# A fused attention and mixture-of-experts kernel: other landing times and due times in its planner, and a second half for the buffer of the attention sums

## The chip, the cores and the metric

The kernel runs on one core of a Trainium2 chip. The metric is the device time of one execution in microseconds (us). The kernel before has a median of 1803.69 us in three runs (1797.37 to 1806.76).

## The reference, cut to what matters

The input x is 8 sequences (the kernel calls each a batch n) of 1024 tokens with 256 features, all in float32. One pre-norm transformer layer is computed:

```
x = x + attention(layernorm(x))      # 16 heads of 16, causal softmax, probabilities times a gate per key
x = x + ffn(layernorm(x))            # 8 experts of width 128, two chosen per token, plus shared experts of width 256

attention: Q, K, V = x@Wq+bq, x@Wk+bk, x@Wv+bv
           gate = tanh(gelu(gelu(norm(x@dp_w1)) @ dp_w2 ...) ...)   # one number per key
           out = (softmax(mask(Q K^T / 4)) * gate) V ; out @ Wo + bo
ffn:       scores = sigmoid(x @ gate_w.T); 4 groups of 2 experts; the best 2 groups; the best 2 experts of these
           y = sum over the two of weight * (silu(x w1) * (x w3)) w2 ; plus the shared experts
```

## The kernel before, in words

Work is cut by batch (n, 8), by group of four heads (g, 4) and by half of the sequence (c, 2 "chunks" of 512 queries). The stages of a batch are: projection (layer norm on DVE, POOL and ACT, transposes and the Q, K and V products on PE), the gate, and for each group first the row maxima of the scores (items M, on DVE the reduce at L1549 and L1546), then the scores again with the maximum subtracted (QK, L1941), their exponential on ACT (EX, L1358), the causal mask on POOL (MK, L1175) and the sums over keys (PV, L1961). The maxima go through a small transfer (SM, L972) into the query tile. Sums are copied from PSUM to `o_sb` by ACT (OE, L1369) and stored to DRAM by SP (SO, L978). After the four groups of a half the row sums are loaded (CL, L986), inverted, stored (CV, L990), and quarters of 256 tokens are loaded (CO, five transfers, L1004 to L1007), multiplied on POOL (CP, L1184), projected (CW, L1970), normalised (CS to CN), transposed (CT, L1978) and handed to the router (CG, L1993), the shared experts and the chosen experts (EU L2071, HT L2081, ED L2102). Tokens are scattered to slots of their experts by indirect transfers from POOL (SX, L1207), slots are loaded in pairs (XL, L1023), worked on, copied to `ysb` by ACT (YC, L1448) and stored (YS, L1033). At the end each tile of 128 tokens gathers its two results (GY, L1219), loads the rest (RL, L1042, tile `rr`), is scaled on ACT (CM, L1294), added on POOL (CB L1227, CC L1232) and stored (SY, L1046). The last batch has no slots: every expert runs on every quarter.

Nothing of this order is written out by hand. `Plan.run` draws it up before the program is built. Every item is added by `plan_work` with its engine, its duration in ns, the items it comes after, its due time and, for a transfer, `lands`: the time from the end of its issue to the point where the plan lets others use the data. The plan goes through time; on each engine it takes, of the items that could start now, the one with the earliest due time. Each engine then runs its items strictly in that order and waits on semaphores, so an order that rested on a landing that comes later than planned makes an engine wait with other work queued behind. `LATER` adds a number of ns to the due time of each kind of item. PE has three ways of tiling (FULL 128x128, ROWS 64x128 for M and QK, COLS 128x32 for PV). The plan charges `SWITCH` for a change of tiling, and `EXPOSED` more unless the new one is COLS; an item in another tiling than the last has `SAME_TILING` added to its due time, so that items of one tiling are kept together. [...] Where the plan sees PE idle with sums open, `keep_busy` puts small matmuls (L858).

```
HEARD = {"PE": {"PE": 0, "ACT": 37, ...}, ...}       # ns until another engine sees an item's end
ISSUE = 620                                          # ns of one transfer's issue on SP
seen[item] = now + ns + (TAIL[e] if lands is None else lands)
cost = [f[1] + (SAME_TILING if f[2] and f[2] != tiling else 0) for f in found]
```

`rank_op` (L1604 to L1615) gives each of n values its rank among n: it compares all with all in a cube of tiles x n x n, five DVE instructions one after the other. `choose_op` calls it twice, for 4 group scores and for 8 expert scores; once per batch for 8 tiles, and in the last batch once per quarter for 2 tiles.

Of the kernel before, what the change touches and what calls it, by code (L numbers as in the profile page):

```python
# [79 lines left out]
RANK_OP = 13  # L80
# [20 lines left out]
DENSE_OPS = 19  # L101
# [8 lines left out]
SWITCH, EXPOSED = 100, 90  # L110
PERIOD, KEEPS = 3413, 0.58
SAME_TILING = 12000
# [65 lines left out]
def max_parts(u):  # L178
# [3 lines left out]
    for qt in qts:  # L182
# [7 lines left out]
LATER = {"AC": 8000, "AQ": -1000, "AX": 7000, "CB": 6000, "CC": -41000, "CG": 3000, "CJ": 2000, "CL": -8000,  # L190
# [138 lines left out]
def plan_work():  # L329
# [11 lines left out]
    def projection(n):  # L341
# [3 lines left out]
        for h in range(HALVES):  # L345
# [3 lines left out]
                lands=4500 if n else 2600, early=70_000 if n == 1 else 0)  # L349
# [59 lines left out]
    def maxima(n, g):  # L409
# [3 lines left out]
        for c in range(CHUNKS):  # L413
# [74 lines left out]
    def quarter(n, q):  # L488
# [4 lines left out]
        if q % (QS // CHUNKS) == 0:  # L493
            early = at(n + 1) - (GROUP_T * 0.4 if c == 0 else 0)
            add("SP", ("CL", n, c), ISSUE, early, [("SO", n, g, c) for g in range(GROUPS)] + [("CV", n - 1, c)], lands=3500)
            add("DVE", ("CR", n, c), 980, early, [("CL", n, c)])
            add("SP", ("CV", n, c), ISSUE, early, [("CR", n, c)], lands=2600)
# [30 lines left out]
        add("SP", ("SR", n, q), ISSUE, begin + 9000, [("FD", n, q)], lands=3500)  # L528

    def routing(n):  # L530
        begin = at(n + 1) + T * SHARE_TO - 10000
        for r, step in enumerate(ROUTE[n]):
            ns = 620 if step in range(9, RANK_OP + 1) else 150
# [10 lines left out]
    def pair(n, u):  # L544
# [4 lines left out]
        add("SP", ("XL", n, u), ISSUE, due - 6000, [("SX", n, 2 * TILES - 1), ("XT",) + back], lands=3500)  # L549
# [6 lines left out]
        add("SP", ("YS", n, u), ISSUE, due + 3500, [("YC", n, u)], lands=3000)  # L556

    def mix(n):
        last = SETS[SET_OF[n]][-1]
        begin = pair_due(last, PAIR_COUNT[last]) + T * MIX_LONG * SETS[SET_OF[n]].index(n)  # L560
        for t in range(TILES):
# [3 lines left out]
            add("SP", ("RL", n, t), ISSUE, due - 3000, [("SR", n, t // QT), ("SY",) + back], lands=2600)  # L565
# [4 lines left out]
            add("SP", ("SY", n, t), ISSUE, due, [("CC", n, t)], lands=2600)  # L570
# [60 lines left out]
def build(nc, ins, out):  # L631
# [4 lines left out]
    with ExitStack() as ctx:  # L636
# [75 lines left out]
        o_sb = sb("o_sb", [P, CHUNK])  # L712
# [14 lines left out]
        cmp_b = sb("cmp_b", [P, TILES, EXPERTS, EXPERTS])  # L727
# [12 lines left out]
        slot_f = sb("slot_f", [P, 2, TILES])  # L740
        slot_u = sb("slot_u", [P, 4, 2, TILES], mybir.dt.uint32)
        owner, owner_old = sb("owner", [P, SLOT_TILES]), sb("owner_old", [P, SLOT_TILES])
        owner_i = sb("owner_i", [P, 2, SLOT_TILES], mybir.dt.int32)
        share = sb("share", [P, 2, TILES])
# [134 lines left out]
        def _(sp):  # L879
# [95 lines left out]
            def store_o(item, n, g, c):  # L975
                b, k = release["OE", n, g, c]
                sp.wait_ge(freed[b], k)
                sp.dma_start(o_s[bass.ds((n * GROUPS + g) * P, P), c * CHUNK:(c + 1) * CHUNK], o_sb[:]).then_inc(o_st[c], 16)  # L978
# [270 lines left out]
        def _(act):  # L1249
# [110 lines left out]
            def copy_o(item, n, g, c):  # L1360
# [8 lines left out]
                nc.scalar.copy(o_sb[:], bank(("PV", n, g, first))).then_inc(freed[release[item][0]], 1)  # L1369
# [95 lines left out]
        def _(dve):  # L1465
# [135 lines left out]
            def rank_op(r, v, n_v, to, ts):  # L1601
                a, b_ = cmp_a[:, ts, 0:n_v, 0:n_v], cmp_b[:, ts, 0:n_v, 0:n_v]
# [8 lines left out]
                if r == 2:  # L1611
                    return nc.vector.tensor_tensor(b_, other, mine, ALU.is_gt)
                if r == 3:
                    return nc.vector.tensor_tensor(a, a, b_, ALU.add)
                return nc.vector.tensor_reduce(to, a, X_AXIS, ALU.add)  # L1615

            def choose_op(r, ts):
# [9 lines left out]
                if r < 8:  # L1627
                    return rank_op(r - 3, grp[:, ts, :], EXPERTS // 2, rank_g[:, ts, :], ts)
                if r == 8:
# [4 lines left out]
                return rank_op(r - 9, sel[:, ts, :], EXPERTS, rank[:, ts, :], ts)  # L1634
# [15 lines left out]
            def slot_op(n, step):  # L1650
# [58 lines left out]
                return nc.vector.tensor_copy(slot_u[:, n % 4, :, :], slot_f[:])  # L1709

            def owner_op(n, step):
# [10 lines left out]
                if step in ("owner_old", "owner"):  # L1722
                    return nc.vector.tensor_reduce((owner_old if step == "owner_old" else owner)[:], ends, X_AXIS, ALU.add)
                if step == "within":
                    return nc.vector.scalar_tensor_tensor(out=owner_old[:], in0=owner_old[:], scalar=float(EXPERTS),
                                                          in1=owner_old[:], op0=ALU.is_lt, op1=ALU.mult)
                if step == "both":
                    return nc.vector.tensor_tensor(owner[:], owner[:], owner_old[:], ALU.add)
# [416 lines left out]
```

## Time and profile before

| | before |
|---|---|
| runs, median (lowest to highest) | 1803.69 us (1797.37 to 1806.76) |
| the profiled execution | 1808.59 us |
| its span on the core | 1806.6 us |
| mean granted TensorE clock | 0.962 of full |
| PE busy | 1653.0 us, 91% of the span |
| DVE, ACT, POOL busy | 1292.4, 1081.9, 811.8 us (72%, 60%, 45%) |
| all transfers | 261.25 MB, mean 145 GB/s |

The span is the time from the first to the last instruction of the profiled execution; 2.0 us lie around it. Busy is the time in which an engine has an instruction in work. The chain that ended last is read backwards: from the last instruction to what released it, and so on; of the span 54% of that chain are PE's, 14% DVE's, 8% each those of transfers, ACT and POOL, 5% issue. A piece of the chain called DMA starts when its transfer is issued and ends when it has landed.

### The profile page before, as it was taken

What the parts mean: (1) busy time and instruction counts of PE and PEld (TensorE: products, weight loads), DVE (VectorE), ACT (ScalarE), POOL (GpSimd) and SP (SyncE); (2) the same over time, 40 slices, a digit from 0 to 9 for tenths busy, and PEclk for the clock granted to TensorE, in tenths of its full rate; (3) what the DMA queues carried; (4) which work ended last, traced back from release to release, by engine and by line L of the source; (5) the groups of instructions that cost most, each with busy time, mean ns of one, the idle gap of its engine ahead of it and who ended that gap; (6) DMA issues with size and microseconds to landing.
All of it is one profiled execution on the core that took longest, in us unless ns stands there. A gap on an engine that the chain in (4) does not pass through costs nothing.

```text
span 1806.6 us, 34673 instructions
## 1 busy us (share of the span) xinstructions
PE 1653.0 (91%) x12785; PEld 982.5 (54%) x12785; DVE 1292.4 (72%) x2528; ACT 1081.9 (60%) x1808; POOL 811.8 (45%) x1390
## 2 busy tenths in 40 slices
PE   7798989989988999899998989999999889999888
PEld 3344446435544566455654555555564557666677
DVE  5776767967795777777785757877688666963655
ACT  3466756665655655675656755586556765568432
POOL 5234533463345221632237863363207773157760
PEclk9699999999998999999998999999999999999999
DMA  5556655554445532644545665453535675336440
GB/s 151 158 156 194 176 169 152 182 153 124 125 127 147 158 104 87 174 113 120 159 118 151 185 194 152 127 162 108 147 93 172 198 197 159 97 129 199 135 122 13
DMA packets 192708, 261.25 MB, mean 145 GB/s; under 512 B 19616, under 2 KB 127264, under 8 KB 192544
## 3 DMA queue, kind: packets, MB, share of 16 engines
q1 hardware_dynamic: 181792, 229.67, 44.0%
q0 software_dynamic: 10752, 29.37, 5.6%
q8 instruction: 105, 1.72, 0.4%
q14 instruction: 59, 0.48, 0.1%
HBM read 130.98 MB, written 127.40 MB: 143 GB/s over the span
## 4 chain that ended last, share of the span: by engine, by line
PE 54%; DVE 14%; DMA 8%; ACT 8%; POOL 8%; issue 5%; SPq 3%; another core or an unknown queue 0%; POOLq 0%; ACTq 0%; DVEq 0%
PE ps_all L1961 10%; PE ps_all L2071 10%; DVE mx L1549 7%; PE ps_all L1941 6%; PE ps_all L1908 6%; PE ps_all L2102 5%; PE ps_all L1892 4%; ACT probs L1358 4%; PE ps_all L1878 3%; PE ps_all L1970 3%; POOL xs_s L1207 2%; PE ps_all L2081 2%; PE ps_all L2034 1%; DMA rr<-r_s 1%; DMA out<-rr 1%
## 5 line engine op out<-in xcount | busy, mean ns | idle before, releaser
L1549 DVE TENSOR_REDUCE mx<-ps_all 128x2 f32<-128x1024 f32 (+2 forms) x640 | 619.0, 1006 | 132.5 <-PE ps_all L1908 74.4
L1358 ACT ACTIVATE probs<-ps_all 128x1024 f32<-128x1024 f32 x576 | 571.8, 1028 | 218.0 <-PE ps_all L1941 209.9
L1175 POOL TENSOR_SCALAR_AFFINE_SELECT probs<-probs 128x256 f32<-128x256 f32 (+1 forms) x448 | 190.9, 443 | 495.5 <-ACT probs L1358 491.3
L1961 PE MATMUL ps_all<-probs,vaug 128*32 128x512 f32 (+3 forms) x3072 | 319.4, 516 | 21.9 <-POOL probs L1175 15.3
L1908 PE MATMUL ps_all<-k_st,q_st 63*128 63x512 f32 (+3 forms) x1536 | 269.3, 401 | 48.0 <-ACT probs L1358 16.3
L1941 PE MATMUL ps_all<-q_st,k_st 64*128 64x512 f32 (+3 forms) x1536 | 265.6, 401 | 29.3 <-ACT probs L1358 9.9
L1908 PEld LDWEIGHTS ps_all<-k_st,q_st 63*128 63x128 f32 x1536 | 135.1, 193 | 163.7 <-issue 52.2
L1941 PEld LDWEIGHTS ps_all<-q_st,k_st 64*128 64x128 f32 x1536 | 130.9, 191 | 158.9 <-issue 67.2
L2071 PE MATMUL ps_all<-w_hi,x2h 128*128 128x512 f32 (+1 forms) x480 | 168.2, 350 | 4.3 <-DVE x2l L1598 2.5
L1804 DVE SCALAR_TENSOR_TENSOR act_t<-act_t,ps_all 128x256 f32<-128x256 f32 x168 | 70.4, 419 | 123.4 <-ACT act_t L1421 110.9
L2071 PE MATMUL ps_all<-w_lo,x2h 128*128 128x512 f32 (+1 forms) x480 | 157.0, 327 | 0.0
L2071 PE MATMUL ps_all<-w_hi,x2l 128*128 128x512 f32 (+1 forms) x480 | 157.0, 327 | 0.0
L1421 ACT ACTIVATE act_t<-ps_all 128x256 f32<-128x256 f32 x168 | 64.6, 385 | 151.3 <-PE ps_all L2071 122.2
L1961 PEld LDWEIGHTS ps_all<-probs,vaug 128*32 128x32 f32 x3072 | 73.2, 110 | 131.6 <-issue 89.4
L1207 POOL DMA_INDIRECT xs_s<-xnb,slot_u x112 | 111.6, 996 | 42.9 <-issue 39.8
L1219 POOL DMA_INDIRECT yab<-ys_s,slot_u x112 | 108.3, 967 | 33.0 <-issue 20.2
L2102 PE MATMUL ps_all<-w_hi,h_hi 128*128 128x256 f32 (+1 forms) x336 | 109.5, 326 | 7.7 <-DVE h_lo L1831 6.9
L2071 PEld LDWEIGHTS ps_all<-w_hi,x2h 128*128 128x128 f32 x480 | 90.8, 189 | 27.6 <-issue 19.7
L1878 PE MATMUL ps_all<-wvd,xt 128*128 128x384 f32 x256 | 96.9, 506 | 1.8 <-issue 0.9
L2071 PEld LDWEIGHTS ps_all<-w_hi,x2l 128*128 128x128 f32 x480 | 90.9, 189 | 8.4
L1831 DVE TENSOR_TENSOR h_lo<-ps_all,h_hi 128x256 fp32r<-128x256 f32 x168 | 70.0, 419 | 35.1 <-ACT h_hi L1436 32.7
L2102 PE MATMUL ps_all<-w_lo,h_hi 128*128 128x256 f32 (+1 forms) x336 | 94.3, 281 | 0.0
(195 smaller groups left out, 2849.8 us busy)
## 6 DMA issues: line engine op xcount, KB each, us to landing
qk_s<-qh SPq DMA_DIRECT2D x116, 256.0 KB
q_st<-qk_s SPq DMA_DIRECT2D x128, 192.0 KB
k_st<-qk_s SPq DMA_DIRECT2D x128, 192.0 KB
xs<-xs_s SPq DMA_DIRECT2D x72, 256.0 KB
ys_s<-ysb SPq DMA_DIRECT2D x72, 256.0 KB
o_s<-o_sb SPq DMA_DIRECT2D x64, 256.0 KB
qk_s<-ql SPq DMA_DIRECT2D x57, 256.0 KB
xs_s<-ysb SPq DMA_DIRECT2D x20, 512.0 KB, 6.0
```

Of the source, the lines that this page charges most:

```text
L1175: last = nc.gpsimd.affine_select(out=block, in_=block, compare_op=ALU.is_ge, fill=0.0, base=0, pattern=[[0, heads], [1, P]], channel_multi ...
L1207: nc.gpsimd.indirect_dma_start(xs_s[i % 2], bass.IndirectOffsetOnAxis(ap=slot_u[:, n % 4, a, t:t + 1], axis=0), xnb[:, t, :], None).then_i ...
L1219: nc.gpsimd.indirect_dma_start(yab[:, t % 2, a, :], None, ys_s[SET_OF[n] % 2], bass.IndirectOffsetOnAxis(ap=slot_u[:, n % 4, a, t:t + 1], ...
L1358: nc.scalar.activation(to, of, ACT.Exp, scale=DH ** -0.5).then_inc(freed[release[item][0]], 1)
L1549: last = nc.vector.tensor_reduce(to[:, :, p, qt % QPC], both[:, :, at:at + keys], X_AXIS, ALU.max)
L1878: last = mm(bank(item)[:, 0:E + DP], xt[:, k, tt * P:(tt + 1) * P], wvd[:, k, :], start=(k == 0), stop=(k == KE - 1))
L1892: last = mm(bank(item), w[:, k, m * P:(m + 1) * P], xt[:, k, :], start=(k == 0), stop=(k == KE - 1))
L1908: last = mm(bank(item, j)[:, to:to + keys], q_st[r, q_half(n, g, c), p, qt % QPC * P:(qt % QPC + 1) * P], k_st[r, k_half(n, g, kc), p, 0:k ...
L1941: last = mm(bank(item, j)[:, to:to + cols], k_st[r, k_half(n, g, kt // QPC), a, kt % QPC * P:(kt % QPC + 1) * P], q_st[r, q_half(n, g, c), ...
L1961: last = mm(bank(first)[32 * h:32 * h + 32, q0 - c * CHUNK:], vaug[:, kt, g, h * VW:h * VW + 32], probs[:, s % 2, h, at:at + cols], start= ...
L2071: last = mm(bank(item)[:, to], x[:, buf, k, t * P:(t + 1) * P], w[:, k, cs], start=(k == 0 and j == 0), stop=(k == KE - 1 and j == 2))
L2102: last = mm(bank(first)[:, t * E:(t + 1) * E], h[:, z % 2, i * P:(i + 1) * P], w[:, cs], start=(item == first and i == 0 and j == 0), stop ...
```

## The change

It has four parts.

1. Constants of the plan. `lands` of nine kinds of transfer goes up: x (AX) 4500 to 5500, maxima (SM) 2600 to 3600, sums (SO) 6000 to 6400, row sums in (CL) 3500 to 4600 and out (CV) 2600 to 3600, rest out (SR) 3500 to 4500, slots in (XL) 3500 to 5200, slots out (YS) 3000 to 4600, rest in and result out (RL, SY) 2600 to 4300. A change of tiling costs 114 instead of 100 and 104 instead of 90 ns more, `SAME_TILING` is 14000 instead of 12000, `KEEPS` 0.6 instead of 0.58.
2. `LATER` has other numbers, and 35 more kinds of item in it (77 in place of 42); among the larger moves: the gate (GA, GD) 13 and 10 us earlier, RL 10 earlier, SY and CL 12 earlier, CC 10 earlier, SM 12 later, XL 10 later, GL 21 later, WF 18 later. The order of the work on all five engines comes out of these two parts.
3. `o_sb` has two halves, one per chunk. The copy of a half waits for the store of the same chunk one group earlier, instead of for the store just before it.
4. `rank_op` reduces each comparison by itself and adds the small results: six instructions in place of five, so that `cmp_b` needs two tiles in place of eight; `slot_f`, `share` and `owner_old` lie in `cmp_a` and `cmp_b`. That makes room for the half of part 3.

```diff
-RANK_OP = 13
+RANK_OP = 15
-DENSE_OPS = 19
+DENSE_OPS = 21
-SWITCH, EXPOSED = 100, 90
-PERIOD, KEEPS = 3413, 0.58
-SAME_TILING = 12000
+SWITCH, EXPOSED = 114, 104
+PERIOD, KEEPS = 3413, 0.6
+SAME_TILING = 14000
-LATER = {"AC": 8000, "AQ": -1000, "AX": 7000, "CB": 6000, "CC": -41000, "CG": 3000, "CJ": 2000, "CL": -8000,
+LATER = {"AB": 8000, "AC": 15000, "AE": 22000, "AG": -1000, "AN": 4000, "AQ": -1000, "AR": -5000, "AS": -1000,
...
-                lands=4500 if n else 2600, early=70_000 if n == 1 else 0)
+                lands=5500 if n else 2600, early=70_000 if n == 1 else 0)
-            add("SP", ("SM", n, g, c), 2 * ISSUE, due, [("MN", n, g, c)], lands=2600)
+            add("SP", ("SM", n, g, c), 2 * ISSUE, due, [("MN", n, g, c)], lands=3600)
-                [("SO", (u - 1) // (GROUPS * CHUNKS), (u - 1) // CHUNKS % GROUPS, (u - 1) % CHUNKS)] if u else []),
+                [("SO", (u - 2) // (GROUPS * CHUNKS), (u - 2) // CHUNKS % GROUPS, c)] if u >= CHUNKS else []),
-            add("SP", ("SO", n, g, c), ISSUE, due + 4000, [("OE", n, g, c)], lands=6000)
+            add("SP", ("SO", n, g, c), ISSUE, due + 4000, [("OE", n, g, c)], lands=6400)
...
-        add("SP", ("YS", n, u), ISSUE, due + 3500, [("YC", n, u)], lands=3000)
+        add("SP", ("YS", n, u), ISSUE, due + 3500, [("YC", n, u)], lands=4600)
-            add("SP", ("RL", n, t), ISSUE, due - 3000, [("SR", n, t // QT), ("SY",) + back], lands=2600)
+            add("SP", ("RL", n, t), ISSUE, due - 3000, [("SR", n, t // QT), ("SY",) + back], lands=4300)
-            add("SP", ("SY", n, t), ISSUE, due, [("CC", n, t)], lands=2600)
+            add("SP", ("SY", n, t), ISSUE, due, [("CC", n, t)], lands=4300)
...
-        o_sb = sb("o_sb", [P, CHUNK])
+        o_sb = sb("o_sb", [P, CHUNKS, CHUNK])
-        cmp_b = sb("cmp_b", [P, TILES, EXPERTS, EXPERTS])
+        cmp_b = sb("cmp_b", [P, 2, EXPERTS, EXPERTS])
...
-                if c:
-                    act.wait_ge(o_st[0], (gi + 1) * 16)
-                else:
-                    act.wait_ge(o_st[1], gi * 16)
+                if gi:
+                    act.wait_ge(o_st[c], gi * 16)
...
                 if r == 2:
-                    return nc.vector.tensor_tensor(b_, other, mine, ALU.is_gt)
+                    return nc.vector.tensor_reduce(to, a, X_AXIS, ALU.add)
                 if r == 3:
-                    return nc.vector.tensor_tensor(a, a, b_, ALU.add)
-                return nc.vector.tensor_reduce(to, a, X_AXIS, ALU.add)
+                    return nc.vector.tensor_tensor(a, other, mine, ALU.is_gt)
+                if r == 4:
+                    return nc.vector.tensor_reduce(others, a, X_AXIS, ALU.add)
+                return nc.vector.tensor_tensor(to, to, others, ALU.add)
```

## Rows read from the trace of the kernel before

**Rows 1.** The page, part 1: busy us of each engine (share of the span) xinstructions.

```profile
PE 1653.0 (91%) x12785; PEld 982.5 (54%) x12785; DVE 1292.4 (72%) x2528; ACT 1081.9 (60%) x1808; POOL 811.8 (45%) x1390
```

**Rows 2.** Who PE's matmuls waited for: us in total, times, longest us.

```profile
PE ps_all L1908 <- ACT probs L1358: 16.3, 30, 1.9
PE ps_all L1908 <- DVE mx L1549: 14.5, 31, 1.9
PE ps_all L1941 <- ACT probs L1358: 9.9, 26, 1.6
PE ps_all L1941 <- DVE mx L1549: 9.7, 19, 1.9
```

**Rows 3.** Timeline, stalls of PE and two of other engines: start us, us, ..., idle before and releaser.

```profile
249.61 0.95 DVE L1561 RECIPROCAL rows_of<-rows_of 64x128 f32<-64x128 f32 x1 [3.98 <-DMA rows_of<-o_s]
...
251.88 0.80 PE L1941 MATMUL ps_all<-q_st,k_st 64*128 64x512 f32 x2 [1.85 <-DVE mx L1549]
...
1043.83 0.91 ACT L1294 ACTIVATE yab<-yab,wab 128x256 f32<-128x256 f32 x2 [4.19 <-DMA yab<-ys_s,slot_u]
...
1045.03 0.50 PE L1908 MATMUL ps_all<-k_st,q_st 63*128 63x512 f32 x2 [1.92 <-DVE mx L1549]
1052.29 0.51 PE L1908 MATMUL ps_all<-k_st,q_st 63*128 63x512 f32 x2 [1.92 <-ACT probs L1358]
...
1666.38 0.36 PE L2102 MATMUL ps_all<-w_hi,h_hi 128*128 x1 [1.75 <-DVE h_lo L1831]
1678.96 1.18 PE L1978 MATMUL ps_all<-ident,xnb 128*128 128x128 f32 x4 [4.86 <-ACT xnb L1315]
1742.51 0.97 PE L1978 MATMUL ps_all<-ident,xnb 128*128 128x128 f32 x3 [2.77 <-ACT xnb L1315]
```

**Rows 4.** The chain that ended last, its transfers there: start us, us until landed.

```profile
242.28 7.31 DMA rows_of<-o_s
...
1044.02 8.95 DMA rr<-r_s
...
1659.48 7.81 DMA ys_s<-ysb
1677.21 5.88 DMA rr<-r_s
1724.44 5.57 DMA rr<-r_s
```

**Rows 5.** Transfers by kind: count, KB each, median us from issue to landing.

```profile
r_s<-x SPq DMA_DIRECT2D x28, 256.0 KB, 2.8
```

**Rows 6.** Stretches: us; PE, PEld, DVE, ACT, POOL busy (x); PE clock, DMA share, GB/s.

```profile
240.00:260.00 20.00, 15.48 (x71) 7.55 (x72) 10.17 (x15) 9.22 (x13) 5.40 (x3) 0.83 0.66 186
...
1040.00:1060.00 20.00, 15.52 (x78) 7.34 (x76) 10.68 (x14) 8.39 (x14) 11.48 (x18) 0.84 0.69 183
...
1660.00:1680.00 20.00, 12.42 (x81) 8.02 (x81) 4.37 (x13) 9.42 (x19) 13.77 (x19) 0.87 0.59 166
...
1740.00:1760.00 20.00, 14.61 (x62) 10.72 (x63) 10.79 (x34) 5.99 (x16) 10.72 (x14) 0.83 0.37 111
```

**Rows 7.** Timeline, a store of the sums and the next copy, closest pair.

```profile
388.66 0.35 SPq L978 DMA_DIRECT2D o_s<-o_sb  x1
396.29 0.59 ACT L1369 COPY o_sb<-ps_all 128x512 f32<-128x512 f32 x1
```

**Rows 8.** DVE groups by form, the add and reduce of the rank: busy us, mean ns.

```profile
L1614 DVE TENSOR_TENSOR cmp_a<-cmp_a,cmp_b 128x512 f32<-128x512 f32 x7 | 4.9, 697 | 0.0
...
L1615 DVE TENSOR_REDUCE rank<-cmp_a 128x64 f32<-128x512 f32 x7 | 4.7, 678 | 0.0
```

**Rows 9.** Timeline of DVE, the same two in the last quarter: start us, us.

```profile
1755.74 1.26 DVE L1614 TENSOR_TENSOR cmp_a<-cmp_a,cmp_b 128x128 f32<-128x128 f32 x1
1757.04 0.29 DVE L1615 TENSOR_REDUCE rank<-cmp_a 128x16 f32<-128x128 f32 x1
```

**Rows 10.** Who PE's weight loads waited for: us in total, times, longest us.

```profile
PEld ps_all L1961 <- issue: 89.4, 320, 1.7
```

More of the change, by code:

```diff
@@ L494, in quarter @@
             early = at(n + 1) - (GROUP_T * 0.4 if c == 0 else 0)
-            add("SP", ("CL", n, c), ISSUE, early, [("SO", n, g, c) for g in range(GROUPS)] + [("CV", n - 1, c)], lands=3500)
+            add("SP", ("CL", n, c), ISSUE, early, [("SO", n, g, c) for g in range(GROUPS)] + [("CV", n - 1, c)], lands=4600)
             add("DVE", ("CR", n, c), 980, early, [("CL", n, c)])
-            add("SP", ("CV", n, c), ISSUE, early, [("CR", n, c)], lands=2600)
+            add("SP", ("CV", n, c), ISSUE, early, [("CR", n, c)], lands=3600)
         back = divmod(k - 2, QS)
@@ L527, in quarter @@
         add("DVE", ("FD", n, q), 600, begin + 9000, [("ED", n, q, quarter_units(n) - 1)], frees=(("ED", n, q, 0), None))
-        add("SP", ("SR", n, q), ISSUE, begin + 9000, [("FD", n, q)], lands=3500)
+        add("SP", ("SR", n, q), ISSUE, begin + 9000, [("FD", n, q)], lands=4500)
     def routing(n):
@@ L532, in routing @@
         for r, step in enumerate(ROUTE[n]):
-            ns = 620 if step in range(9, RANK_OP + 1) else 150
+            ns = 620 if step in range(10, RANK_OP + 1) else 150
             ready = [("RO", n, r - 1)] if r else [("RT", n, QS - 1), ("GY", n - 4, TILES - 1), ("CM", n - 4, TILES - 1)]
@@ L548, in pair @@
         y = look_of(n, QS, u)
-        add("SP", ("XL", n, u), ISSUE, due - 6000, [("SX", n, 2 * TILES - 1), ("XT",) + back], lands=3500)
+        add("SP", ("XL", n, u), ISSUE, due - 6000, [("SX", n, 2 * TILES - 1), ("XT",) + back], lands=5200)
         add("PE", ("XT", n, u), 370, due - 2000, [("XL", n, u)] + look_end(y - 2), 1, FULL)
@@ L1363, in copy_o @@
                     act.wait_ge(pv_done, gi * NSTEP + LAST_STEP[c] + 1)
-                if c:
-                    act.wait_ge(o_st[0], (gi + 1) * 16)
-                else:
-                    act.wait_ge(o_st[1], gi * 16)
+                if gi:
+                    act.wait_ge(o_st[c], gi * 16)
                 first = FIRST_STEP[c]
-                nc.scalar.copy(o_sb[:], bank(("PV", n, g, first))).then_inc(freed[release[item][0]], 1)
+                nc.scalar.copy(o_sb[:, c, :], bank(("PV", n, g, first))).then_inc(freed[release[item][0]], 1)
             def copy_hi(item, n, q, i):
@@ L1601, in rank_op @@
             def rank_op(r, v, n_v, to, ts):
-                a, b_ = cmp_a[:, ts, 0:n_v, 0:n_v], cmp_b[:, ts, 0:n_v, 0:n_v]
+                a, others = cmp_a[:, ts, 0:n_v, 0:n_v], cmp_b[:, 0, 0:ts.stop - ts.start, 0:n_v]
                 cube = [P, ts.stop - ts.start, n_v, n_v]
@@ L1633, in choose_op @@
                         scalar=2.0, in1=sc[:, ts, :].rearrange("p t (g o) -> p (t g) o", o=2), op0=ALU.is_lt, op1=ALU.mult)
-                return rank_op(r - 9, sel[:, ts, :], EXPERTS, rank[:, ts, :], ts)
+                return rank_op(r - 10, sel[:, ts, :], EXPERTS, rank[:, ts, :], ts)
             def spread_op(r, ts):
@@ L1722, in owner_op @@
                 if step in ("owner_old", "owner"):
-                    return nc.vector.tensor_reduce((owner_old if step == "owner_old" else owner)[:], ends, X_AXIS, ALU.add)
+                    return nc.vector.tensor_reduce(owner_old if step == "owner_old" else owner[:], ends, X_AXIS, ALU.add)
                 if step == "within":
-                    return nc.vector.scalar_tensor_tensor(out=owner_old[:], in0=owner_old[:], scalar=float(EXPERTS),
-                                                          in1=owner_old[:], op0=ALU.is_lt, op1=ALU.mult)
+                    return nc.vector.scalar_tensor_tensor(out=owner_old, in0=owner_old, scalar=float(EXPERTS),
+                                                          in1=owner_old, op0=ALU.is_lt, op1=ALU.mult)
                 if step == "both":
-                    return nc.vector.tensor_tensor(owner[:], owner[:], owner_old[:], ALU.add)
+                    return nc.vector.tensor_tensor(owner[:], owner[:], owner_old, ALU.add)
                 return nc.vector.tensor_scalar(owner_i[:, SET_OF[n] % 2, :], owner[:], float(EXPERTS - 1), float(2 * F),
```

14 lines of the change are left out of this document (7 added, 7 removed), and 14 rows, old and new, of the table LATER.

## The prediction

> **What bounds the kernel now.** I read the page first, then PE's waits, then the timeline around its longest stalls, and last the chain of work. The page says that PE is busy 1653.0 of 1806.6 us, far ahead of DVE at 1292.4 [rows 1]. So PE is the bound, and what can be won without taking work from it is its idle time, 1806.6 - 1653.0 = 153.6 us, and the time that it works at a low clock: at a mean granted clock of 0.962 the missing 0.038 is 1806.6 x 0.038 = 69 us. The idle time is not in one place. Of matmul waits, the four largest groups in which PE waits in its M and QK items for a bank that ACT or DVE has yet to empty sum to 16.3 + 14.5 + 9.9 + 9.7 = 50.4 us, in 106 waits of at most 1.9 us [rows 2].
>
> The timeline shows a second kind: an engine stands in its fixed order before a transfer that has not landed, and what is queued behind it comes late. At 249.61 DVE has waited 3.98 us for the row sums; the maxima behind them come late, and PE stalls 1.85 us at 251.88. At 1043.83 ACT has waited 4.19 us for gathered rows, and PE stalls 1.92 us twice soon after. At 1666.38, 1678.96 and 1742.51 PE stalls 1.75, 4.86 and 2.77 us [rows 3]. The chain shows transfers ahead of these: row sums landed 7.31 us after their issue began, a slot store 7.81, and loads of the rest 8.95, 5.88 and 5.57 [rows 4]. The plan of before expected, with 0.62 us of issue, 0.62 + 3.5 = 4.12 us for the first, 0.62 + 3.0 = 3.62 for the second and 0.62 + 2.6 = 3.22 for the others. This is what the change is about.
>
> **The change part by part.**
>
> *Landings.* After the change the plan expects 5.22, 5.22 and 4.92 us for these three kinds. Of the lateness it takes in (5.22 - 4.12) / (7.31 - 4.12) = 34% for the row sums, 1.6 / 4.19 = 38% for the slot store, 1.7 / 2.66 = 64% and 1.7 / 2.35 = 72% for the loads of the rest at 1677 and 1724 us [rows 4]. I let PE's stall behind each shrink by that share: 1.85 x 0.34 + 1.75 x 0.38 + 4.86 x 0.64 + 2.77 x 0.72 = 0.6 + 0.7 + 3.1 + 2.0 = 6.4 us, of 11.2 [rows 3]. The chain for the last two runs from the load of the rest over POOL's adds (L1227, L1232) and gathers to the layer norm of the quarter, all queued on POOL, and from there to ACT and PE. The two stalls at 1045 and 1052 stand behind a gather (GY), whose landing of 4000 ns is not changed: nothing is counted. Not every raise goes towards the trace: stores of the rest land after a median of 2.8 us, where the plan said 4.12 and now says 5.12 [rows 5]. That costs nothing by itself, since a semaphore is waited for and not a time; it only lets the plan put other work first. Ends: nothing comes back (0), or all 11.2 us.
>
> *The clock behind the stalls.* The stretches from 240, 1660 and 1740 us have granted clocks of 0.83, 0.87 and 0.83; a part of each ran at 1.2 GHz, the lower level, in place of 2.4 GHz, after PE had stood still [rows 6]. 20 us at 0.83 lose 3.4 us of full-speed work, so the three lose 3.4 + 2.6 + 3.4 = 9.4 us. With stalls shorter by 6.4 of 11.2 I take the same share of it, 5.4 us. Ends: 0 and 9.4 us. The stretch from 1040 us, 0.84, belongs to the gather and stays.
>
> *Two halves of the sums' buffer.* Before, the copy at L1369 waits for the store just before it. In all 64 pairs the closest is a store that starts at 388.66 and a copy that starts at 396.29, 7.6 us later, and ACT's idle time before L1369 is never ended by a transfer [rows 7]. So the wait that is removed costs 0 now. The plan, which holds the copy back for 0.62 + 6.0 us, may place it earlier, and with it the bank that it frees; PE's own waits on this copy are under 2 us in all, so I take 0, with 2 us to gain at the other end.
>
> *The rank in six instructions.* Each call gives up one add over the cube and gains a reduce over the same cube and a small add. At 8 tiles the add took 0.697 us and the reduce 0.678 [rows 8]; the small add is taken at the price of the short reduce, 0.29 us [rows 9]. So a call costs -0.02 + 0.29 = +0.27 us, 14 calls in seven batches +3.8 us on DVE, which has over 500 us to spare; it hides beside the maxima, and costs up to 3.8 us where DVE is just then the one PE waits for. In the last batch, 8 calls, the add over 2 tiles took 1.26 us and the reduce 0.29 while POOL was at work [rows 9], so a call gives back 1.26 - 0.58 = 0.68 us there and costs 0.3 where POOL is quiet. Sum on the path: 0, ends -5 and +4. On this pair of rows the Trainium skill has a rule ("SBUF — State Buffer", Who interferes with whom): a DVE instruction with two inputs in SBUF contends with a GpSimd instruction that reads SBUF, a reduce on trn2 does not. By it the part would be on the side of the gain, about -0.7 us in the only place where the router's chain holds PE; it changes the sum by less than 1 us.
>
> *Due times, costs of tiling and of the clock.* These reorder all engines: SP's queue (row sums, loads of the rest and results earlier, maxima later), POOL's (second add and the gate earlier) and ACT's. No work goes away. What is left of PE's idle time is 153.6 - 11.2 = 142 us, and a new order draws it anew. No row says in which direction. I take 0, with a fifth of it, 30 us, as the bound on either side: less than the 50.4 us of waits for banks [rows 2], which a new order moves first.
>
> Sum against the profiled execution: 1808.6 - 6.4 - 5.4 + 0 + 0 + 0 = 1796.8 us. It lies 4.9 us above the median of the three runs, so the forecast for the median is 1791.9, rounded to 1791 us.
>
> **The rivals.**
>
> *A. The stalls only move (no change).* PE's order is as rigid as before. Where the plan now allows for a landing of a row sum or a load, another kind whose landing is as low as it was (the gather, or the stores of Q and K) becomes the late one. For it: the wait of 4.19 us before the gather's use [rows 3]. Against it: at the three places that I count it is the raised kinds that lead the chain. It gives 1808.6 - 4.9 = 1804, 1795 to 1812.
>
> *B. Longer runs in one tiling (slower).* With 14 in place of 12 us of preference for the present tiling PE does more M or QK items in a row. One M item's PE time is about 0.5 us, its two reduces on DVE more than 1 us, so that each further item of a run waits for a bank. The place is the four groups of [rows 2]. If they grow by 80%, 40 us come on top, and the time is 1792 + 40 = 1832; the point from which it decides is a growth by (1804 - 1792) / 50.4 = 24%, over which the gain is eaten; at 50% it gives 1817. For it: these waits are the largest group already. Against it: the same plan counts the banks and sees a wait for them coming.
>
> *C. Fewer changes of tiling (a larger gain).* The timeline has some 1080 changes between the three tilings, the first at 37 us and the last at 1672 us. Before the PV items PE's weight loads stood still for 89.4 us in 320 waits with no releaser, 0.28 us each [rows 10]. If the new costs take away 10% of the changes, that is up to 108 x 0.28 = 30 us, and the time is 1762. Against it: much of that idle lies beside a matmul still running. The Trainium skill ("TensorEngine Tiling (Array Packing)", Key Properties) says that a change of the tiling mode drains the engine, which speaks for a full price of each change; no row here separates the drain.
>
> *D. The change does not do what it says.* The second half changes nothing where the wait was never met [rows 7]. That is in my sum already; if the landings were no cause either, the result is A.
>
> **How the numbers follow.** A measurement of this kernel can tell about 0.5%, 9 us, from no change: the bounds are 1794.7 and 1812.7. My forecast gets 0.43 (its own range 1780 to 1799: 0.35 of it under 1794.7, 0.08 within), C and a lucky redraw 0.19 (1755 to 1780), A 0.16 (within), B 0.22 (1813 to 1835). Faster by over 0.5%: 0.35 + 0.19 = 0.54; within: 0.08 + 0.16 = 0.24; slower: 0.22. For the range I leave out about a third of C at the lower end and half of B at the upper: 1768 to 1817. The likeliest case's own range is 1780 to 1799.
>
> **What would show it.** If I am right, the profile of the changed kernel has the stalls of PE before L1978 near the end shorter than 4.86 and 2.77 us, POOL's waits for loads of the rest and DVE's for row sums smaller in total, a granted clock of 0.965 or more, PE's busy time within 10 us of 1653, and no wait of ACT at L1369 for a transfer. A is right if these waits shrink and others grow by as much; B if the four groups of [rows 2] exceed 62 us; C if the weight loads' waits with no releaser before L1961 fall under 80 us. I am wrong if the redraw of all orders, which I put at 0, is the largest term: then the idle time of PE changes by more than 15 us with no landing at the head of it.

## The result, and the profile after

The changed kernel takes 1788.28 us (median of 11 runs, 1778.47 to 1798.91) against 1800.42 us for the kernel before (11 runs, 1793.26 to 1809.04). The ratio is 0.993, with a 95% interval of 0.9902 to 0.9959. A second measurement of the same program beside the kernel before (e9) gave 0.9928 (0.9902 to 0.9953). So the change is faster by 0.7%, near the 1791 us forecast; how much of that is owed to the reasons that I gave is what the experiments are about.

| | before | after |
|---|---|---|
| median of all runs | 1800.42 us | 1788.28 us |
| profiled execution | 1808.59 us | 1798.91 us |
| its span | 1806.6 us | 1797.1 us |
| PE busy, PE idle | 1653.0, 153.6 us | 1650.4, 146.7 us |
| granted clock | 0.962 | 0.968 |

Both profiled executions are slower than their medians, the changed one by 10.6 us: it was the slowest of its 11. The profile of e9, the same program again, has a span of 1785.3 us, PE busy 1640.7 and a clock of 0.971, and I name its numbers beside those of the first where they matter.

The page of the changed kernel, part 1, answers [rows 1]:

```profile
PE 1650.4 (92%) x12770; PEld 979.4 (54%) x12770; DVE 1288.9 (72%) x2550; ACT 1079.7 (60%) x1808; POOL 810.5 (45%) x1390
```

The span fell by 9.5 us: 6.9 us less idle time of PE and 2.6 us less busy time. The busy time holds the plan's small filler matmuls too, which compute nothing. They are 15 fewer, all of the difference in PE's records. Before (first line) and after, busy us, mean ns:

```profile
L858 PE MATMUL ps_all<-bars,scan 128*64 128x512 bf16 x135 | 42.9, 408 | 0.0
```

```profile
L862 PE MATMUL ps_all<-bars,scan 128*64 128x512 bf16 x120 | 37.5, 408 | 0.0
```

So the time in which PE does nothing of the computation, idle and fillers together, fell from 153.6 + 42.9 = 196.5 to 146.7 + 37.5 = 184.2 us, and the busy time of the computation itself did not fall: 1610.1 before, 1612.9 after. In e9 the two are 181.9 and 1603.4 us. (These sums are estimates, since a matmul's record can overlap the next one's.)

Who PE's matmuls waited for in the changed kernel (L1912 and L1945 are the M and QK items, L1908 and L1941 before), us in total, times, longest us; the first four answer [rows 2]:

```profile
PE ps_all L1912 <- ACT probs L1362: 14.5, 33, 1.4
PE ps_all L1945 <- ACT probs L1362: 11.8, 23, 2.7
PE ps_all L1912 <- DVE mx L1551: 7.9, 25, 0.5
...
PE ps_all L1945 <- DVE mx L1551: 5.2, 12, 1.6
...
PE ps_all L1982 <- ACT xnb L1319: 3.2, 2, 2.5
```

The four groups of waits for a bank sum to 14.5 + 11.8 + 7.9 + 5.2 = 39.4 us, against 50.4 before [rows 2]; in e9 to 38.0. It is DVE's part that shrank, from 24.2 to 13.1 us. That alone is more than the whole fall of the idle time. The waits for the normalised rows (L1982) fell to 3.2 us in total; before they were:

```profile
PE ps_all L1978 <- ACT xnb L1315: 8.9, 4, 4.9
```

Who the other engines waited for in the changed kernel, transfers only:

```profile
POOL oc L1188 <- DMA x<-in_x: 63.4, 20, 7.9
...
POOL rr L1231 <- DMA rr<-r_s: 11.6, 5, 3.5
...
ACT yab L1298 <- DMA yab<-ys_s,slot_u: 7.1, 5, 2.7
...
DVE rows_of L1563 <- DMA rows_of<-o_s: 1.7, 1, 1.7
```

and in the kernel before:

```profile
POOL oc L1184 <- DMA x<-in_x: 35.4, 15, 6.2
...
POOL rr L1227 <- DMA rr<-r_s: 33.8, 11, 7.4
...
ACT yab L1294 <- DMA yab<-ys_s,slot_u: 21.3, 15, 4.2
...
DVE rows_of L1561 <- DMA rows_of<-o_s: 11.5, 6, 4.0
```

The waits for the rest (`rr`), for gathered rows (`yab`) and for row sums (`rows_of`) were 66.6 us in all; now they are 20.4, and in e9 24.4. In return POOL waits 63.4 us for x in place of 35.4. The stall before the last quarters' transposes, 4.86 and 2.77 us in [rows 3], is 2.48 us once:

```profile
1674.31 0.93 PE L1982 MATMUL ps_all<-ident,xnb 128*128 128x128 f32 x4 [2.48 <-ACT xnb L1319]
```

and the stretches that answer [rows 6] (columns as there) show the clock at 1.00, 0.98, 0.91 and 0.99 in place of 0.83, 0.84, 0.87 and 0.83:

```profile
240.00:260.00 20.00, 19.66 (x124) 11.29 (x122) 15.12 (x29) 10.63 (x19) 3.94 (x6) 1.00 0.46 132
1040.00:1060.00 20.00, 19.86 (x136) 12.71 (x134) 12.70 (x28) 12.98 (x29) 13.47 (x18) 0.98 0.53 159
1660.00:1680.00 20.00, 15.33 (x105) 9.80 (x104) 5.25 (x14) 11.77 (x24) 17.08 (x25) 0.91 0.55 171
1740.00:1760.00 20.00, 17.55 (x94) 14.11 (x94) 16.80 (x53) 7.35 (x22) 10.16 (x14) 0.99 0.33 99
```

On this page alone my theory looks proven: the late transfers are waited for less, the clock is better where I said, and the time fell by what I had said.

### The profile page after: what moved, and what is told of

Same layout as the page of the kernel before. It is cut to its first block, busy times and chain, and to the rows that moved or that the text cites. A ratio compares the mean times of both kernels' runs of the same rounds, so it can differ in the third digit from the quotient of the medians.

```text
span 1797.1 us, 34689 instructions
## 1 busy us (share of the span) xinstructions
PE 1650.4 (92%) x12770; PEld 979.4 (54%) x12770; DVE 1288.9 (72%) x2550; ACT 1079.7 (60%) x1808; POOL 810.5 (45%) x1390
## 4 chain that ended last, share of the span: by engine, by line
PE 53%; DVE 13%; ACT 10%; POOL 7%; DMA 7%; issue 5%; SPq 4%; another core or an unknown queue 1%; POOLq 0%; DVEq 0%; ACTq 0%
PE ps_all L2075 10%; PE ps_all L1965 10%; DVE mx L1551 6%; PE ps_all L1945 6%; PE ps_all L1912 6%; PE ps_all L2106 5%; ACT probs L1362 5%; PE ps_all L1896 4%; PE ps_all L1882 3%; PE ps_all L1974 2%; POOL xs_s L1211 2%; DMA qk_s<-ql 2%; PE ps_all L2085 1%; PE ps_all L1997 1%; DMA x<-in_x 1%
## 5 line engine op out<-in xcount | busy, mean ns | idle before, releaser
L1965 PE MATMUL ps_all<-probs,vaug 128*32 128x512 f32 (+3 forms) x3072 | 323.0, 517 | 29.4 <-POOL probs L1179 18.9
L1912 PE MATMUL ps_all<-k_st,q_st 63*128 63x512 f32 (+3 forms) x1536 | 267.3, 399 | 41.0 <-ACT probs L1362 14.5
L1945 PE MATMUL ps_all<-q_st,k_st 64*128 64x512 f32 (+3 forms) x1536 | 262.3, 401 | 26.8 <-ACT probs L1362 11.8
L1912 PEld LDWEIGHTS ps_all<-k_st,q_st 63*128 63x128 f32 x1536 | 133.2, 190 | 162.7 <-issue 53.3
L1945 PEld LDWEIGHTS ps_all<-q_st,k_st 64*128 64x128 f32 x1536 | 128.9, 191 | 148.7 <-issue 65.6
L1965 PEld LDWEIGHTS ps_all<-probs,vaug 128*32 128x32 f32 x3072 | 72.3, 111 | 139.1 <-issue 96.9
L1438 ACT CAST h_hi<-ps_all 128x256 fp32r<-128x256 f32 x168 | 60.3, 374 | 63.9 <-PE ps_all L2085 57.0
L2075 PEld LDWEIGHTS ps_all<-w_lo,x2h 128*128 128x128 f32 x480 | 92.8, 193 | 5.6
```

Source lines behind the costliest of these rows:

```text
L1912: last = mm(bank(item, j)[:, to:to + keys], q_st[r, q_half(n, g, c), p, qt % QPC * P:(qt % QPC + 1) * P], k_st[r, k_half(n, g, kc), p, 0:k ...
L1945: last = mm(bank(item, j)[:, to:to + cols], k_st[r, k_half(n, g, kt // QPC), a, kt % QPC * P:(kt % QPC + 1) * P], q_st[r, q_half(n, g, c), ...
L1965: last = mm(bank(first)[32 * h:32 * h + 32, q0 - c * CHUNK:], vaug[:, kt, g, h * VW:h * VW + 32], probs[:, s % 2, h, at:at + cols], start= ...
L2075: last = mm(bank(item)[:, to], x[:, buf, k, t * P:(t + 1) * P], w[:, k, cs], start=(k == 0 and j == 0), stop=(k == KE - 1 and j == 2))
```

## The experiments

All twelve have intervals of about 0.2 to 0.4% on either side. They ran on three chips: e1 to e4 on one, e5 to e8 on another, e9 to e12 on a third; on which chip the result was taken is not on record. Each ratio is to the kernel before on the same chip. It is the recorded ratio with its interval, and not the quotient of the two medians, which can differ from it by 0.2% (for e9 1788.26 / 1804.12 = 0.991, recorded 0.9928).

### The change in two halves (e1, e2)

e1 has all of the change but the due times, of which it has the 42 of before:

```diff
-LATER = {"AB": 8000, "AC": 15000, "AE": 22000, ...
+LATER = {"AC": 8000, "AQ": -1000, "AX": 7000, ...
```

> All of the change but the new due times: the raised landings, the costs of tiling and of the clock, the two halves and the rank in six instructions, with the due times of before. If the landings bring the gain (my theory), it keeps most of it: ratio to before 0.990 to 0.997, POOL's waits for loads of the rest under 20 us (33.8 before). If the due times bring it, the ratio is 0.998 to 1.005. If constants and due times only fit each other, it is slower than before: 1.005 or more.

It took 1801.88 us, ratio 1.0059 (1.0037 to 1.0082): slower than before. e2 has the reverse, the new due times with the landings and costs of before (the landings of all ten kinds, restored too, are left out of the lines):

```diff
-SWITCH, EXPOSED = 114, 104
-PERIOD, KEEPS = 3413, 0.6
-SAME_TILING = 14000
+SWITCH, EXPOSED = 100, 90
+PERIOD, KEEPS = 3413, 0.58
+SAME_TILING = 12000
...
```

> The new due times, the halves and the rank, with the landings and the costs of tiling and clock of before. If the landings bring the gain, ratio to before 0.998 to 1.004 and POOL's waits for loads of the rest above 25 us. If the due times bring it, 0.990 to 0.996. If both only fit each other, 1.005 or more.

It took 1785.86 us, ratio 0.9965 (0.9946 to 0.9984). The profiles show where my theory falls short. Who waited in e1:

```profile
POOL rr L1227 <- DMA rr<-r_s: 20.0, 10, 4.5
...
ACT yab L1294 <- DMA yab<-ys_s,slot_u: 9.4, 9, 2.4
...
DVE rows_of L1559 <- DMA rows_of<-o_s: 1.0, 1, 1.0
```

and whom PE waited for in e1:

```profile
PE ps_all L1908 <- DVE mx L1547: 16.9, 39, 1.3
PE ps_all L1941 <- ACT probs L1358: 16.2, 22, 4.9
PE ps_all L1908 <- ACT probs L1358: 15.3, 34, 2.3
PE ps_all L1941 <- DVE mx L1547: 10.7, 19, 2.1
...
PE ps_all L1978 <- ACT xnb L1315: 3.9, 2, 3.1
```

The constants do what they are for, at the places for which I had counted on them. The three waits for transfers are 30.4 us, from 66.6 before and 54.6 in e4, which has the same due times and rank but not the constants. The wait before L1978 is 3.9 us, from 8.9. The three stretches from which I took the clock's term are better too, 1.00, 1.00 and 0.91 in place of 0.83, 0.87 and 0.83:

```profile
240.00:260.00 20.00, 16.31 (x121) 8.20 (x121) 11.01 (x19) 9.91 (x13) 9.58 (x14) 1.00 0.85 268
...
1660.00:1680.00 20.00, 18.48 (x133) 12.31 (x133) 5.93 (x13) 14.17 (x26) 15.09 (x21) 1.00 0.53 171
1740.00:1760.00 20.00, 16.48 (x86) 12.51 (x85) 12.63 (x40) 7.53 (x20) 13.93 (x18) 0.91 0.45 138
```

But the waits for a bank are 59.1 us, against 48.3 in e4:

```profile
PE ps_all L1908 <- ACT probs L1358: 21.3, 34, 3.9
...
PE ps_all L1908 <- DVE mx L1547: 10.1, 29, 0.8
PE ps_all L1941 <- DVE mx L1547: 8.5, 17, 1.7
PE ps_all L1941 <- ACT probs L1358: 8.4, 24, 1.3
```

and the time is not lower. e1 raises the landings and the costs of tiling together, so no run says which of the two brought these waits back. In e2 the waits for transfers are still there:

```profile
POOL rr L1231 <- DMA rr<-r_s: 17.8, 8, 6.5
...
ACT yab L1298 <- DMA yab<-ys_s,slot_u: 23.1, 13, 4.0
...
DVE rows_of L1563 <- DMA rows_of<-o_s: 11.7, 4, 5.8
```

They are 52.6 us, and the waits for a bank are as many as in e4, 48.6 us:

```profile
PE ps_all L1912 <- DVE mx L1551: 14.9, 36, 2.8
PE ps_all L1912 <- ACT probs L1362: 13.7, 32, 3.6
...
PE ps_all L1945 <- ACT probs L1362: 11.0, 27, 2.5
PE ps_all L1945 <- DVE mx L1551: 9.0, 13, 5.4
```

and yet the kernel is faster. The pair on one chip with the old constants, e4 and e2 (1.0037 and 0.9965), which differ in the due times alone, gives the new due times 0.7%, with intervals that do not meet. Constants on top of old due times: 1.0037 to 1.0059, intervals that overlap. Constants on top of new due times: 0.9965 to 0.993, which overlap too, and on different chips. So the due times carry what can be measured here, and the constants by themselves carry no gain. Whether it is what the due times say, or only that they draw another order, this pair cannot tell.

### The second half and the rank (e3, e4, e12)

e3 takes the second half of the buffer out of the changed kernel, in the plan and in the wait:

```diff
-        o_sb = sb("o_sb", [P, CHUNKS, CHUNK])
+        o_sb = sb("o_sb", [P, CHUNK])
...
-                if gi:
-                    act.wait_ge(o_st[c], gi * 16)
+                if c:
+                    act.wait_ge(o_st[0], (gi + 1) * 16)
+                else:
+                    act.wait_ge(o_st[1], gi * 16)
```

> The changed kernel with one buffer for the sums again, in the plan and in the wait; the rest as changed. My theory has the second half at 0 to 2 us: ratio to before 0.992 to 0.996, no wait of ACT's copy for a transfer. A rival, that the half lets the plan place the copies earlier and so frees banks, loses the gain: 0.998 or more. The order is drawn anew by it, so a difference of less than 0.4% from the changed kernel decides nothing.

1791.71 us, ratio 0.9994 (0.9975 to 1.0012). The gain is gone. By what I had written beforehand that points to the rival, that the half matters through the plan; but the order was drawn anew. Against my expectation there is also one copy that waits for a transfer, 2.7 us:

```profile
ACT o_sb L1373 <- DMA o_s<-o_sb: 2.7, 1, 2.7
```

e5 (below) prices such a wait without a new order. e4 is the kernel before with parts 3 and 4 of the change alone, planned anew:

> The kernel before with the two halves and the rank in six instructions alone; constants and due times of before. My theory: 0 for both, ratio 0.997 to 1.003. If the half is worth something by itself, 0.996 or less. If the rank costs on the path, 1.003 to 1.005 with DVE busy 2 to 4 us more.

1798.47 us, ratio 1.0037 (1.0014 to 1.006), slower. e12 has the same parts in the order of the kernel before, item for item and bank for bank; the reduce and the small add of the rank are issued as one item:

```diff
+                nc.vector.tensor_reduce(others, a, X_AXIS, ALU.add).then_inc(rank_mid, 1)
+                mids.append(r)
+                dve.wait_ge(rank_mid, len(mids))
+                return nc.vector.tensor_tensor(to, to, others, ALU.add)
```

> The kernel before with its order on every engine and its banks kept as they are, and in it the two halves and the rank in six instructions (the last two issued as one item). It prices parts 3 and 4 without a new order. My prediction had 0 with ends of -7 and +4 us: ratio 0.998 to 1.002. If the rank's extra instructions cost on the path, 1.003 or more, as with the order drawn anew (1.0037); if the half helps, 0.997 or less.

1807.20 us against 1804.12, ratio 1.0026 (1.0006 to 1.0046). My sum had 0 with an end at +4 us for the rank; 0.26% is 4.7 us, with 1 and 8 us as the ends of the interval (the two medians are 3.1 us apart). Its DVE groups by form show what was added:

```profile
L1615 DVE TENSOR_REDUCE cmp_b<-cmp_a 128x64 f32<-128x512 f32 x7 | 4.7, 675 | 0.0
...
L1618 DVE TENSOR_TENSOR rank<-rank,cmp_b 128x64 f32<-128x64 f32 x7 | 1.8, 257 | 0.2
```

The reduce that takes the place of the add lasts 0.675 us (the add took 0.697, [rows 8]), and the small add 0.257, against the 0.29 that I took. DVE is busy 2.2 us more (1294.6 against 1292.4). So the prices of one instruction were right. As for the path, the measurement excludes 0 by little and holds both the 2.2 us of added DVE time and my end of +4 us: it fits with all of it lying on the path, which I had put at 0. Whether it is the rank chain, the new wait inside it or the looser wait of the copies, e12 does not separate.

### The wait alone, in the changed order (e5, e9, e10, e11)

e5 keeps the changed kernel's order and both halves, but each copy waits for the store just before it:

```diff
-                if gi:
-                    act.wait_ge(o_st[c], gi * 16)
+                if c:
+                    act.wait_ge(o_st[0], (gi + 1) * 16)
+                else:
+                    act.wait_ge(o_st[1], gi * 16)
```

> The changed kernel with its order on every engine kept as it is, but the copy of the sums waits for the store just before it, as in the kernel before (two halves, one wait). It prices the wait alone. In the changed profile the closest copy starts 5.9 us after the start of the store before it, all others 8.6 us or more, so my theory says 0 to 1 us: ratio to before 0.991 to 0.995. A rival in which the wait itself matters gives 0.998 or more.

It came out at 1770.36 us, ratio 0.9878 (0.9841 to 0.9915): a stricter wait, and apparently faster than the changed kernel on another chip (0.993). I had no mechanism for this. The timeline shows the one copy for which the stricter wait counts. In the changed kernel:

```profile
231.02 0.47 SPq L982 DMA_DIRECT2D o_s<-o_sb  x1
...
236.96 0.59 ACT L1371 COPY o_sb<-ps_all 128x512 f32<-128x512 f32 x1 [2.76 <-PE ps_all L1965]
```

and in e5, where the copy waits until the store that began at 230.65 has landed, 6.7 us later:

```profile
230.65 0.47 SPq L982 DMA_DIRECT2D o_s<-o_sb  x1
...
237.38 0.59 ACT L1373 COPY o_sb<-ps_all 128x512 f32<-128x512 f32 x1 [4.63 <-DMA o_s<-o_sb]
...
238.02 1.73 PE L1898 MATMUL ps_all<-xt,wk 128*128 128x512 f32 x3 [2.77 <-ACT o_sb L1373]
```

PE then waits 2.77 us for the bank. So I ran three kernels side by side on a third chip: the changed one (e9), the changed one with only this one wait made stricter (e10), and e5 again (e11).

```diff
+                if gi == 4 and c == 0:
+                    act.wait_ge(o_st[1], gi * 16)
-                if gi:
+                elif gi:
                     act.wait_ge(o_st[c], gi * 16)
```

> The changed kernel itself, on the same chip as the next three. It measured 0.993 of before (interval 0.990 to 0.996) on another chip: expected 0.991 to 0.995. If that gain was the chip's, 0.997 to 1.000.

> The changed kernel with its order kept and one single wait made stricter: the ninth copy of the sums, which started 5.9 us after the store before it, waits for that store. My theory that waits cost what they last gives the changed kernel's time plus 0 to 3 us. If the frozen order with stricter waits was faster because of this one delay, which shifts all that follows, it repeats that time: ratio to before 0.984 to 0.990.

> The changed kernel's order with every copy waiting for the store just before it, once more, beside the changed kernel on one chip. If the 0.988 was the chip's, it comes out equal to the changed kernel within 0.3%; if it belongs to the kernel, 0.985 to 0.990 again, 0.3 to 0.8% under the changed kernel.

They took 1788.26, 1785.58 and 1790.73 us, ratios 0.9928, 0.9907 (0.9877 to 0.9936) and 0.993 (0.9903 to 0.9958): equal. The 0.9878 does not come back on another chip, for the same program. So one copy made to wait costs nothing that can be measured at the end, and the ratio of a program to the kernel before may differ from chip to chip by about 0.5%. That difference is barely clear of noise, since the two intervals overlap between 0.9903 and 0.9915; why it is there, no run here shows. For e3 it means that the half is worth nothing as a wait, and that what e3 lost, it lost by its new order. Whether it lost it because the half no longer lets the plan place copies earlier, or because any new draw would have lost it, is not separated; the next three runs show that a new draw alone can lose as much.

### Other draws of the order (e6, e7, e8)

If the due times make the difference, is it their direction or this one order? e6 and e7 add 1 us to, or take it from, each of the 77 due times of the changed kernel, by lot; e8 does so with the 42 of the kernel before.

```diff
-LATER = {"AB": 8000, "AC": 15000, "AE": 22000, "AG": -1000, "AN": 4000, ...
+LATER = {"AB": 7000, "AC": 14000, "AE": 23000, "AG": -2000, "AN": 5000, ...
```

> The changed kernel with 1 us added to or taken from the due time of each of the 77 kinds, by lot. If the gain comes from landings and costs that fit the chip, it stays: ratio to before 0.989 to 0.997. If the order of the changed kernel is only one lucky draw of many, the gain goes: 0.999 to 1.008.

> The same with another lot: 0.989 to 0.997 if the gain is the constants', 0.999 to 1.008 if it is a draw. The two together show how far one draw lies from another.

> The kernel before with 1 us added to or taken from each of its 42 due times, by lot. If its order is an ordinary draw, ratio to before 0.996 to 1.004; if it is a chosen one, as a draw theory of both kernels says, 1.003 to 1.012.

e6 took 1790.30 us, ratio 0.9998 (0.9974 to 1.0022), e7 1794.51 us, 1.0013 (0.9992 to 1.0034), and e8 1811.67 us, 1.0113 (1.0081 to 1.0146). Beside e5, which has the order of the changed kernel on the same chip, e6 and e7 are 1.1% and 1.4% slower by their medians. A lot of 1 us, small against due times moved by 10 to 20 us in the change, takes away all of the gain, and makes the kernel before 1.1% slower. All three neighbours that I tried are slower than the order they were drawn from, so both orders look chosen. In e7 the waits for a bank are back:

```profile
PE ps_all L1912 <- DVE mx L1551: 18.0, 37, 4.5
...
PE ps_all L1945 <- ACT probs L1362: 16.1, 31, 5.5
PE ps_all L1912 <- ACT probs L1362: 15.2, 35, 1.3
...
PE ps_all L1945 <- DVE mx L1551: 7.2, 13, 2.4
...
PE ps_all L1982 <- ACT xnb L1319: 1.8, 2, 1.3
```

56.5 us, while the wait before L1982 is smaller than in the changed kernel. All kernels together, in groups by chip, with the waits of each profile in us. The clock is the mean over all runs of a kernel. "Not computing" is PE's idle time and its fillers together.

| | constants | ratio | clock | PE not computing | three waits for transfers | wait for normalised rows | four waits for a bank |
|---|---|---|---|---|---|---|---|
| before (profile of the result) | old | 1 | | 196.5 | 66.6 | 8.9 | 50.4 |
| after (profile of the result) | new | 0.993 | 0.9730 | 184.2 | 20.4 | 3.2 | 39.4 |
| *first chip, before's clock 0.9688* | | | | | | | |
| e2, new due times | old | 0.9965 | 0.9689 | 184.1 | 52.6 | 7.2 | 48.6 |
| e3, one half | new | 0.9994 | 0.9682 | 184.7 | 27.8 | 3.5 | 43.5 |
| e4, parts 3 and 4 | old | 1.0037 | 0.9641 | 194.2 | 54.6 | 6.6 | 48.3 |
| e1, old due times | new | 1.0059 | 0.9672 | 198.6 | 30.4 | 3.9 | 59.1 |
| *second chip, before's clock 0.9687* | | | | | | | |
| e5, after's order | new | 0.9878 | 0.9753 | 168.4 | 29.2 | 3.2 | 36.9 |
| e6, after, by lot | new | 0.9998 | 0.9675 | 184.1 | 43.7 | 1.2 | 47.7 |
| e7, after, by lot | new | 1.0013 | 0.9667 | 175.8 | 39.6 | 1.8 | 56.5 |
| e8, before, by lot | old | 1.0113 | 0.9618 | 206.4 | 48.0 | 7.8 | 50.2 |
| *third chip, before's clock 0.9646* | | | | | | | |
| e10, after's order | new | 0.9907 | 0.9737 | 182.2 | 24.3 | 3.2 | 41.5 |
| e9, after again | new | 0.9928 | 0.9714 | 181.9 | 24.4 | 3.2 | 38.0 |
| e11, after's order | new | 0.993 | 0.9722 | 185.2 | 20.1 | 3.2 | 37.8 |
| e12, parts 3 and 4, old order | old | 1.0026 | 0.9653 | 194.6 | 58.9 | 8.7 | 46.0 |

Three things can be read from it.

The wait for normalised rows follows the constants in every order: 6.6 to 8.9 us with the old ones, 1.2 to 3.9 us with the new ones. So the raised constants do take some 5 us off PE at the place where I had looked for it. The time does not follow: each set of constants has kernels faster than before and slower.

No kind of wait orders the times. The waits for a bank are few in the changed kernel's order and most in e1, but e4 and e2 differ by 0.3 us in them and by 0.7% in time, and e8 has fewer than e7 and is slower by 1%.

What goes with the time, chip by chip, is how long PE does not compute, over all kinds of wait. Only e7 is out of line: the busy time of its computation is 1622.3 us, against 1598 to 1613 in all others. The clock goes with it: in the order of the changed kernel it is higher than before's by 0.007 to 0.009 (e5, e9, e10, e11), in no other by more than 0.001. What the clock by itself is worth can't be read off. Taken at its face, 0.0068 of 1790 us, it would be 12 us in e9, an estimate; but the computation's busy time fell there by 6.7 us only, and rose by 2.8 in the first profile, whose clock is up by 0.006. Nor do the runs show whether the clock makes an order fast, or whether fewer stalls leave it up.

## Why the prediction was right or wrong

*The number.* Forecast 1791 us, a ratio of 1791 / 1803.69 = 0.9930; measured 1788.28 us and 0.993. The direction and the size were right. (The sum came to 1791.9 and rounds to 1792, not to the 1791 that I wrote.) All five signs that I had named for being right came true in the first profile: shorter stalls before the transposes, smaller waits for loads and row sums, a clock over 0.965, PE's busy time within 10 us of 1653, no copy waiting for a transfer. But all five hold in e1 as well (stalls of 3.9 us in total, waits of 20.0 and 1.0 us, 0.966, 1651.2 us, none), and e1 is slower than before. They were signs that the constants act, and none that the time falls by it.

*Landings: the mechanism is there, and its way into the time is not.* I let PE's stalls behind late transfers shrink from 11.2 by 6.4 us. The stalls before the transposes near the end did: 8.9 us of waits in total became 3.2 in the changed kernel and 3.9 in e1. That is close to the 5.1 us that the steps for the load of the rest had. The step that failed is the silent one after it, that PE's idle time falls by what one kind of stall loses: against e4 that kind is 2.7 us less in e1 and the waits for a bank are 10.8 us more, and PE's idle time is 155.1 us in place of 153.4. This is my rival A for the constants taken alone, with another kind of wait than I named there; the raised costs of tiling may have a part in it (rival B). I had expected of e1 that it keeps most of the gain, and it is slower than before. The claim that the gather's wait (GY) stays because its landing is not changed did not hold: it is 7.1 us in the changed kernel and 9.4 in e1, from 21.3, and 15.2 to 23.1 in e7, e6 and e2. It goes by the order and not by its own landing.

*The clock.* I took 5.4 us, at most 9.4, from three stretches of [rows 6], by the share of the stalls that the landings take away. The three stretches improved as I said, and the fourth, from 1040 us, that I had left at 0.84, went to 0.98. The step from there to the time failed: in e1 the same three stretches are at 1.00, 1.00 and 0.91, and yet the mean over its runs, 0.9672, is no better than before's 0.9688. The mean did go up in the changed order, by 0.007, but in none of the four other orders with the same constants (e1, e3, e6, e7). So the clock's gain, whatever its size, belongs to the order and not to the landings.

*The second half.* 0 was right for the wait, which was never the last: the changed kernel without it in the same order (e11) is equal to the changed kernel (e9). In the changed order there is one copy, at 236.96 us, that a single buffer would hold up; it costs nothing at the end. What it is worth to the plan stays open (e3).

*The rank.* 0 predicted, with ends of -5 and +4; parts 3 and 4 in the order of before measured +4.7 us (e12, 1 to 8 us). The prices per instruction were right at 8 tiles. The end of -5 us came from one row: the add of 1.26 us in [rows 9] is the longest of the eight in the last batch, whose others took 0.18 to 0.78 us. The step in doubt is that the extra work hides behind DVE's idle time. I found no wait in e12's profile that shows the path, and the new wait inside the chain is in the same run, so where it enters stays open.

*Due times at 0, with 30 us to either side.* This is the term that carried the result. e4 and e2 differ in it alone and by 0.7%, 13 us; two lots around the changed kernel lose the whole gain, one lot around the kernel before loses 1.1%, 20 us. I had written that I would be wrong if the redraw of all orders were the largest term, "then the idle time of PE changes by more than 15 us with no landing at the head of it". The idle time changed by less, 6.9 us, and still it was the largest term, since an order also moves the fillers, the busy time and the clock (the time in which PE does not compute fell by 12.3 us). So the number is right in part by luck. The 11.8 us that I took off for landings and clock are not there in e1, which has these constants and is slower; about 13 us that I had at 0 came with the due times instead.

*The rivals.* B (longer runs in one tiling) named the waits for a bank; in the changed kernel they fell, 39.4 in place of 50.4 us. In e1, where the costs of tiling meet the old due times, it goes the way B says: 59.1 us, 17% over the 50.4, under the 24% at which I let it decide, and the kernel is slower than before by 0.6%, the rank's part included. Since no run has the costs of tiling without the landings, B is not refuted for that kernel. C (fewer changes of tiling) is not borne out. Counted in the timelines, there are 1086 changes between the three tilings, from 1082 before (1084 in e1), and the weight loads' waits with no releaser grew from 89.4 [rows 10] to 96.9 us:

```profile
PEld ps_all L1965 <- issue: 96.9, 329, 2.7
```

D was right on the wait and is part of the sum.

## What to carry to other kernels

When an order is drawn up by a planner, a change of its constants is two changes: the corrected model, and a new draw of everything else. Measure some neighbours of both orders (here 1 us by lot on each due time, at 0.7 to 1.1% each) before a gain of that size is put down to the correction. A kind of wait that shrinks in a profile is no gain by itself: add up all the time in which the engine that sets the end does nothing of the computation, fillers included, before and after. And of a sign that is to confirm a theory, ask beforehand whether it would also show if the theory's cause acts and the time does not follow; all five of mine did.

## What the runs showed of the hardware

The same program gave 0.9878 (0.9841 to 0.9915) of the kernel before on one chip and 0.993 (0.9903 to 0.9958) on another, each beside runs of the kernel before on that chip. The kernel before itself has medians of 1792.49, 1792.47 and 1804.12 us on the three chips (35, 23 and 18 runs), with mean clocks of 0.9688, 0.9687 and 0.9646. For differences of half a per cent, kernels that are to be compared with each other belong on one chip.

One and the same program does not run at one clock: the 11 runs of the changed kernel have mean granted clocks of 0.968 to 0.978, and the slowest of them, 1798.91 us, is the one profiled here, at 0.968. That is 0.005 under the mean of the 11, most of the 0.007 by which the changed order gains.

Work added to an engine with idle time need not be free: DVE is idle for 28% of the span, and the few instructions more of e12, 2.2 us of DVE's busy time, came with 4.7 us (1 to 8). That run also has a new wait in the chain and a looser one at the copies, so the cost is not shown to be DVE's alone.
